# A two-layer network on one core: the second layer's experts in engine loops, its tokens sorted in three parts, with eight weight and row buffers

## The chip, the cores and the metric

The kernel runs on one core of a Trainium2 chip. Its time is the device time of one execution in microseconds (us); smaller is better. The engines are TensorE (PE in the profile, its weight loads PEld), VectorE (DVE), ScalarE (ACT), GpSimd (POOL) and SyncE (SP), which here only issues transfers. Each engine runs its own instruction stream in order and waits on semaphores.

## The reference

Two layers run on a tensor x of 8 x 512 tokens with 128 features, 4096 tokens in all. Layer 0 is a recurrent scan over every second token and a small mixture of experts; layer 1 is an attention with 16 heads and relative positions and then a larger mixture of experts. Only that last part is touched. Cut to what matters:

```python
h = _layernorm(x) * (1 + cb) + sb
# _L1_ffn_ref, 8 experts, the best 2 of each token, and one shared expert for all
scores = softmax(xt @ gate_w.T)
idx = top_k(scores + gate_b, 2)[1]
weights = take_along_axis(scores, idx)
cw = sum(one_hot(idx, 8) * weights[..., None], axis=1)
h1 = einsum('td,efd->etf', xt, w1) + b1
h3 = einsum('td,efd->etf', xt, w3) + b3
a = swiglu(h1 * h3)          # g * sigmoid(1.702 g) * (l + 1) on even and odd columns, clipped at 7
y = einsum('etf,edf->etd', a, w2) + b2
routed = einsum('te,etd->td', cw, y)
shared = swiglu((xt @ sw1.T + sb1) * (xt @ sw3.T + sb3)) @ sw2.T + sb2
x = x + gb * (routed + shared)
```

All is float32.

## The kernel before

`program` runs the stages one after the other. The last one is `experts1` (L1397). It does not compute all 8 experts for all tokens. It sorts: each token's two (token, expert) pairs get a slot in a buffer in HBM, ordered by expert, and the experts run over blocks of `SLOTS` = 256 slots that all belong to one expert.

**Routing.** VectorE makes softmax, the two maxima and the running counts, and from these the slot of every pair (`pos`, L1698) and the expert of every block (`eid`). The 32 tiles of 128 tokens are sorted in `PARTS` = 2 parts of `PT` = 16 tiles (2048 tokens). A part has at most `RB` = 2*16*128/256 + 7 = 23 blocks, since each of the 8 experts may leave one block unfilled. So 46 routed blocks run, always, beside `NSHARED` = 16 blocks of the shared expert, which need no sorting: N = 62.

**Order.** `ORDER` puts 11 shared blocks first, then the 46 routed ones, then the last 5 shared ones. All engines follow it; their code is written out block by block.

**GpSimd** scatters the rows of `norm.h` to `sorted_h` with one indirect DMA for each tile and each of its two experts (64 in all, L1565). For each part it then waits until all its results are stored and gathers them to `got` the same way (32 for each part, L1574). A ring of `NGOT` = 4 semaphores lets it run four tiles ahead of their landing.

**SyncE** serves the routed blocks. For block m it first issues the rows of block m + 1 (`load_slots`, L1525, 128 KB, `NX` = 4 buffers), then reads the expert's number into a register (L1516) and issues the weights of block m (`load_weights`, L1517, 320 KB, `NW` = 5 buffers, free when block m - 5 has left `down`), then stores the result of block m - 5 (`store`, L1531, 128 KB).

**One block** is a pipeline over four engines. TensorE: `turn` (two transposes of the rows, L1829), `up` (four matmuls of 256 columns, L1842 to L1851, to one PSUM bank each), and two blocks later `down` (L1866; for shared blocks also L1865, the output bias). ScalarE: `slots` (L1592), `gate` (L1598), `tanh` (L1610), `lin` (L1604), `take` (L1621). VectorE: `gates` (L1725, L1728), `join` of the block before (L1742, L1748), `lins` (L1733, L1736). `select_biases` (L1709 to L1720) picks the first biases of all routed blocks on VectorE, once, at block 4.

**The end.** `combine(k)` (L1754) adds the two gathered rows of tile k, weighted, to `acc`: two operations of 128 x 128. Eight tiles of part 0 are combined between the blocks, one every second block; the other 24 after the last block, with `finish` (L1760, L1762) for every four tiles, and SyncE stores each of the eight pieces of the output (L1546).

## Time and profile before

| | us |
|---|---|
| median of 3 runs (1836.76 to 1840.22) | 1839.58 |
| the profiled execution | 1833.77 |
| its span, first to last instruction | 1832.0 |
| its granted TensorE clock, mean | 0.877 |

The shares of the whole span say little here, since the stages have different limits. `experts1` is its last 390 us or so. What is of use is a table of stretches (busy time of each engine, the clock granted to TensorE, the share of the DMA engines), the number of blocks in each, and single instructions in order of time where an engine stands still. In a row of the timeline the bracket tells how long the engine had been idle and what released it; "remote" means that a semaphore changed at that moment, and that no instruction of that moment had changed it.

### The profile page before, as it was taken

The numbers are of one execution on the slowest core, as the hardware profiler recorded it, in microseconds if no ns is written. First come the engines' busy times: TensorE is split into PE (matmuls) and PEld (weight loads), VectorE is DVE, ScalarE is ACT, GpSimd is POOL, SyncE is SP. The second block draws the span as 40 slices with busy tenths as digits, with TensorE's granted clock in tenths as the row PEclk, the third lists the DMA queues.
The fourth block names the chain that finished last, engine by engine and source line by source line (L and its number), as shares of the span: only waits on it lengthen the run. The fifth ranks groups of instructions, "written<-read, shape, count | busy, mean of one in ns | idle before, by whom it ended". The sixth has DMA issues, their size and how long they took to land. (4 is left out here: it accounts for less than half of the span.)

```text
span 1832.0 us, 41747 instructions
## 1 busy us (share of the span) xinstructions
PE 1461.2 (80%) x15040; PEld 996.7 (54%) x15040; DVE 1314.7 (72%) x3621; ACT 952.3 (52%) x2202; POOL 592.0 (32%) x584
## 2 busy tenths in 40 slices
PE   4277767776698569999999999999999577198490
PEld 2277667776643235555555555555555455187370
DVE  6899999997678736667666676666766685077286
ACT  7555555554311436666666666666666432066260
POOL 0876666770113334111111111111110107601415
PEclk7688888888699789999999999999999867599695
DMA  2400000000000012111111111111110001258352
GB/s 70 132 1 1 1 1 1 1 1 0 12 1 5 15 22 42 31 29 30 29 30 26 25 30 28 30 30 30 30 28 8 15 1 54 71 154 231 95 140 82
DMA packets 150357, 71.53 MB, mean 39 GB/s; under 512 B 95234, under 2 KB 135700, under 8 KB 150164
## 3 DMA queue, kind: packets, MB, share of 16 engines
q1 hardware_dynamic: 143316, 60.42, 15.1%
q0 software_dynamic: 4096, 8.40, 1.5%
q8 instruction: 106, 1.74, 0.4%
q14 instruction: 87, 0.71, 0.1%
q10 hardware_dynamic: 2752, 0.26, 0.1%
HBM read 38.11 MB, written 18.35 MB: 31 GB/s over the span
## 5 line engine op out<-in xcount | busy, mean ns | idle before, releaser
L1299 DVE TENSOR_REDUCE ntop<-score 128x1 f32<-128x512 f32 x512 | 317.9, 683 | 252.0 <-PE score L1178 252.0
L1256 ACT ACTIVATE prob<-score,ntop 128x512 f32<-128x512 f32 x512 | 317.5, 688 | 268.6 <-DVE ntop L1299 268.6
L440 ACT ACTIVATE hist<-zp 128x168 f32<-128x168 f32 (+1 forms) x768 | 224.4, 313 | 171.1 <-DVE zp L408 170.4
L1214 PE MATMUL turned<-ident,prob 128*128 128x128 f32 x2048 | 268.5, 280 | 1.8 <-DVE probT L1240 1.8
L490 PEld LDWEIGHTS py<-hist,diagC 128*128 128x128 f32 x2048 | 262.6, 214 | 0.0
L490 PE MATMUL py<-hist,diagC 128*128 128x128 f32 x2048 | 262.3, 296 | 0.0
L1178 PE MATMUL score<-ks,qs 64*128 64x512 f32 x1024 | 255.0, 616 | 0.0
L1214 PEld LDWEIGHTS turned<-ident,prob 128*128 128x128 f32 x2048 | 219.0, 141 | 49.1 <-issue 28.1
L460 POOL TENSOR_TENSOR xb<-xc,Bm 128x1024 f32<-128x1024 f32 x128 | 244.9, 1954 | 1.3
L403 DVE TENSOR_TENSOR gp<-hist,Ap 128x168 f32<-128x168 f32 (+1 forms) x768 | 229.7, 328 | 14.8 <-POOL xb L460 14.8
L408 DVE TENSOR_TENSOR zp<-gp,xb 128x168 f32<-128x168 f32 (+1 forms) x768 | 232.9, 333 | 0.0
L1240 ACT COPY probT<-turned 128x512 f32<-128x512 f32 x384 | 198.7, 595 | 1.2 <-PE turned L1214 1.2
L1178 PEld LDWEIGHTS score<-ks,qs 64*128 64x128 f32 x1024 | 88.5, 186 | 168.8 <-issue 168.8
L931 POOL TENSOR_TENSOR qr<-rel_q,own_shift 128x256 f32<-128x256 f32 x64 | 37.3, 615 | 403.9 <-PE score L1178 373.0
L1174 PE MATMUL score<-tb,qr 32*32 32x512 f32 x4096 | 148.6, 603 | 12.4 <-PEq L946 11.7
L1198 PEld LDWEIGHTS mixed<-probT,vh 128*16 128x16 f32 x4096 | 100.7, 96 | 95.8 <-issue 95.8
L1198 PE MATMUL mixed<-probT,vh 128*16 128x128 f32 x4096 | 136.4, 274 | 0.7 <-issue 0.7
L938 POOL TENSOR_TENSOR qs<-key_q,own_batch 128x256 f32<-128x256 f32 x128 | 95.6, 792 | 73.5 <-DMA key_q<-q_sb 73.5
L1574 POOL DMA_INDIRECT got<-sorted_y,pos x64 | 61.9, 966 | 160.5 <-DMA sorted_y<-ysb 141.6
L1286 DVE RECIPROCAL inv<-cm 128x256 f32<-128x256 f32 x64 | 111.5, 1743 | 0.0
L1240 DVE COPY probT<-turned 128x512 f32<-128x512 f32 x128 | 88.5, 691 | 0.1
L1565 POOL DMA_INDIRECT sorted_h<-hz,pos x64 | 63.7, 995 | 55.9 <-DVE pos L1698 36.7
(304 smaller groups left out, 1624.9 us busy)
## 6 DMA issues: line engine op xcount, KB each, us to landing
w<-in_ew SPq DMA_DIRECT2D x46, 320.0 KB
tb<-in_table SPq DMA_DIRECT2D x64, 127.1 KB
sorted_h<-nought SPq DMA_DIRECT2D x2, 2944.0 KB, 17.2
xs<-sorted_h SPq DMA_DIRECT2D x46, 128.0 KB
sorted_y<-ysb SPq DMA_DIRECT2D x46, 128.0 KB
ks<-k_sb SPq DMA_DIRECT2D x32, 128.0 KB
rel_q<-q_sb SPq DMA_DIRECT2D x248, 8.0 KB
key_q<-q_sb SPq DMA_DIRECT2D x248, 8.0 KB
```

What stands on the lines that cost most here:

```text
L403: v.tensor_tensor(g[:, lo:hi], prev[:, lo:hi], Ap[:, lo:hi], ALU.mult).then_inc(decayed, 1)
L408: v.tensor_tensor(zp[j][:, 0:hi - lo], g[:, lo:hi], xb[:, par, u, lo:hi], ALU.add)\
L440: nc.scalar.activation(hist[:, par, u, lo:hi], zp[j][:, 0:hi - lo], ACT.Tanh)\
L460: nc.gpsimd.tensor_tensor(xb[:, par, u:u + XB_STEPS, :].rearrange("p u (s b) -> p u s b", b=NB), xc[:, par, u * NB:(u + XB_STEPS) * NB].re ...
L490: last = mm(py[par][:, 0:P], diagC[:, s, :], hist[:, par, :, s * NB:(s + 1) * NB], start=False, stop=(s == NS - 1))
L1174: mm(score_ps[r][32 * w:32 * w + 32, :], qr[p][rows, w, g, :, :].rearrange("p b v -> p (b v)"), tb[p][rows, s:s + SEQ], start=True, stop=F ...
L1178: mm(score_ps[r][:, :], qs[p][rows, r % 2, g, :, :, :].rearrange("p w b v -> p (w b v)"), ks[p][rows, :], start=False, stop=True).then_inc ...
L1198: last = mm(mixed_ps[32 * c:32 * c + SUMS, bh * P:(bh + 1) * P], vh[:, p, j, b, :], probT[G // 2 % 2][:, j, :, :].rearrange("p t (w b v) - ...
L1214: last = nc.tensor.transpose(turned_ps[BANK[e]][:, j * P:(j + 1) * P], prob[G % 2][e][:, j * P:(j + 1) * P], ident[:, :])
L1240: copy(probT[G // 2 % 2][:, :, G % 2 * GRP + TURN[e], :], turned_ps[BANK[e]][:, :].rearrange("p (j t) -> p j t", j=JT))\
L1256: nc.scalar.activation(prob[G % 2][e][:, :], score_ps[r][:, :], ACT.Exp, bias=ntop[:, G % 2, e:e + 1]).then_inc(prob_ready, 1)
L1299: v.tensor_reduce(ntop[:, G % 2, e:e + 1], score_ps[r][:, :], AX.X, ALU.max, negate=True)\
```

## The change

The change is confined to `experts1`, its constants, and the width of the zeroed buffers; one transfer in `attention` gets another semaphore.

- **Parts.** The tiles are sorted in three parts of 8, 16 and 8 tiles (1024, 2048 and 1024 tokens). `RB` is 15, 23 and 15, so 53 routed blocks run, and N = 69. The running counts are made for groups of 8 tiles in 3 steps and joined for the middle part; their totals come from three small matmuls of their own.
- **Order.** 10 shared blocks first, 53 routed, 6 shared last.
- **SyncE.** Eight weight buffers and eight row buffers. The first 8 loads of weights are issued before any rows; then, for block m, the weights of block m + 8, the store of block m, the rows of block m + 8. The weights land on one semaphore for each group of four.
- **Loops.** TensorE runs blocks 12 to 59 in 6 laps of 8 blocks, ScalarE blocks 4 to 7 in 2 laps and 16 to 59 in 11 laps of 4, VectorE blocks 4 to 61 in laps of 2, five loops with 3 + 15 + 4 + 3 + 4 = 29 laps. Semaphore values and the columns of biases and tiles are worked out in registers.
- **Biases.** The first biases are picked by four small matmuls (`select` on TensorE, at block 2) and one copy on ScalarE.
- **Combines.** Tiles 0 to 7 are combined at blocks 40 to 47, tiles 8 to 15 at blocks 54 to 61, one for every block. Tiles 16 to 31 and all `finish` come after the last block, behind a wait for the last `take`. `NGOT` is 2.

```diff
-PARTS = 2
-PT = NT // PARTS
-RB = 2 * PT * P // SLOTS + NE1 - 1
-NROUTED = PARTS * RB
+QT = 8
+PART_QUARTERS = (1, 2, 1)
+PARTS = len(PART_QUARTERS)
+PT = [QT * q for q in PART_QUARTERS]
+RB = [2 * t * P // SLOTS + NE1 - 1 for t in PT]
+NROUTED = R0[PARTS]
...
-    NW, NX, NY, NGOT = 5, 4, 4, 4
-    SHARED_FIRST, SELECT_AT, IN_LOOP, EVERY = 11, 4, 8, 2
+    NW, WG, NX, NY, NGOT = 8, 4, 8, 4, 2
+    LAP = 8
+    SHARED_FIRST = 10
+    SELECT_AT = 2
...
-            load_slots(0)
-            for m in range(NROUTED):
-                if m + 1 < NROUTED:
-                    load_slots(m + 1)
-                load_weights(m)
-                if m >= AFTER:
-                    store(m - AFTER)
-            for m in range(NROUTED - AFTER, NROUTED):
-                store(m)
+            for m in range(NW):
+                load_weights(m)
+            for m in range(SLOTS_AHEAD):
+                load_slots(m)
+            for m in range(NROUTED):
+                if m + NW < NROUTED:
+                    load_weights(m + NW)
+                store(m)
+                for k in range(SLOTS_AHEAD, NROUTED):
+                    if asked_at(k) == m:
+                        load_slots(k)
...
             for s in range(PARTS):
                 for i in range(NY):
-                    pool.wait_ge(y_out[i], 16 * stores(i, (s + 1) * RB))
-                for k in range(s * PT, (s + 1) * PT):
+                    pool.wait_ge(y_out[i], 16 * stores(i, R0[s + 1]))
+                for k in range(T0[s], T0[s + 1]):
...
+            def stretch(n0, turns, tile=None):
+                with dve.Fori(0, turns) as i:
+                    for u in range(2):
+                        q = (n0 + u) % 2
+                        bias = routed_bias(2 * i + (n0 - SHARED_FIRST + u))
+                        gates(2 * i + (n0 + u), q, bias)
+                        join(2 * i + (n0 - 1 + u), 1 - q)
+                        lins(2 * i + (n0 + u), q, bias)
+                        if tile is not None:
+                            combine(2 * i + (tile + u), (tile + u) % NGOT, i + (tile // NGOT + 1))
...
+            dve.wait_ge(sel_ready, 1)
+            stretch(SHARED_FIRST, 15)
+            dve.wait_ge(y_taken, SHARED_FIRST)
+            stretch(SHARED_FIRST + 30, 4, 0)
+            stretch(SHARED_FIRST + 38, 3)
+            stretch(SHARED_FIRST + 44, 4, 8)
+            for n in range(SHARED_FIRST + 52, N):
+                gates(n, n % 2, bias_of(n))
+                join(n - 1, (n - 1) % 2)
+                lins(n, n % 2, bias_of(n))
+            join(N - 1, (N - 1) % 2)
+            dve.wait_ge(y_taken, N)
+            for k in range(16, NT):
+                combine(k, k % NGOT, k // NGOT + 1)
...
+            with pe.Fori(0, 6) as i:
+                for u in range(LAP):
+                    q = u % 2
+                    turn(LAP * i + (3 + u), (3 + u) % NX, 1 - q, i + ((3 + u) // NX + 1))
+                    up_routed(LAP * i + (12 + u), LAP * i + (2 + u), (2 + u) % NW, q, WG * i + WG * ((2 + u) // NW + 1))
+                    down(LAP * i + (10 + u), q, W[u])
```

Three places of the order show what moves. On VectorE, the end of a routed block with a combine behind it reads like this before (`gg`, `ll`, `a` are the block's tiles, `acc` the sum of a token tile, `got` the gathered rows; the brackets name the semaphores waited for):

```order
L1742 SCALAR_TENSOR_TENSOR ll<-ll,gg 128x256 [waits ll_ready,gg_ready]
L1748 SCALAR_TENSOR_TENSOR a<-th,ll 128x256 [waits y_ready1,th_ready,gl_ready]
L1733 SCALAR_TENSOR_TENSOR ll<-pz,b_sel,l 128x256 [waits first_l]
L1736 TENSOR_SCALAR ll<-ll 128x256 [waits ll_raw]
L1754 SCALAR_TENSOR_TENSOR acc<-got,wt,acc 128x128 [waits got_in0,y_taken]
L1754 SCALAR_TENSOR_TENSOR acc<-got,wt,acc 128x128 [waits combined]
L1725 SCALAR_TENSOR_TENSOR gg<-pz,b_sel,g 128x256 [waits first_g,combined]
```

and like this inside the loop of the changed kernel, up to the end of the combine, where ISA and REGISTER_ALU are register instructions:

```order
L1801 SCALAR_TENSOR_TENSOR a<-th,ll 128x256 [waits y_ready1]
L1787 ISA [waits first_l]
L1787 SCALAR_TENSOR_TENSOR ll<-pz,b_sel,l 128x256
L1790 TENSOR_SCALAR ll<-ll 128x256 [waits ll_raw]
L1807 ISA
L1812 ISA [waits got_in0]
L1812 ISA
L1812 SCALAR_TENSOR_TENSOR acc<-got,wt,acc 128x128
L1813 REGISTER_ALU
L1812 ISA [waits combined]
L1812 SCALAR_TENSOR_TENSOR acc<-got,wt,acc 128x128
L1813 REGISTER_ALU
```

The operations and their order are the same; seven register instructions stand between them in this piece, three of them with a wait. On SyncE, the steady rows for one routed block are before:

```order
L1525 DMA xs3<-sorted_h1 128x2x128 [waits xs_turned]
L1516 TENSOR_LOAD eid [waits y_ready1]
L1516 ISA x2
L1517 ISA
L1517 DMA w1_1<-in_ew1 128x640
L1531 DMA sorted_y0<-ysb1 128x2x128 [waits y_taken]
```

and in the changed kernel:

```order
L1541 TENSOR_LOAD eid [waits y_ready1]
L1541 ISA x2
L1542 ISA
L1542 DMA w1_2<-in_ew1 128x640
L1562 DMA sorted_y1<-ysb2 128x2x128 [waits y_taken]
L1555 DMA xs2<-sorted_h1 128x2x128 [waits xs_turned]
```

The rows are now asked for after the store, and the store is that of the block whose `down` has just ended. On GpSimd, the changed kernel scatters the three parts and begins the gathers of the first, which is of 8 tiles (16 DMAs) now:

```order
L1598 DMA sorted_h0<-hz,pos 3840x128 [waits pos_ready]
L1598 DMA sorted_h0<-hz,pos 3840x128 x15
L1598 DMA sorted_h1<-hz,pos 5888x128 x32
L1598 DMA sorted_h2<-hz,pos 3840x128 x16
L1607 DMA got<-sorted_y0,pos 128x128 [waits y_out2,y_out3,y_out1,y_out0]
L1607 DMA got<-sorted_y0,pos 128x128 x3
L1607 DMA got<-sorted_y0,pos 128x128 [waits got_in0]
L1607 DMA got<-sorted_y0,pos 128x128
L1607 DMA got<-sorted_y0,pos 128x128 [waits got_in1]
```

Before, `sorted_h0` and `sorted_h1` took 32 DMAs each, the first eight gathers waited for no landing, and the ring had four semaphores. Now four gathers (two tiles) start without such a wait.

## Rows read from the trace of the kernel before

**Rows 1.** Stretches, `tanh` alone: us, ACT busy (x, one a block), PEclk, DMA share, GB/s

```profile
1511.00:1537.00 26.00, 2.44 (x6) 0.87 0.14 47
1537.00:1602.50 65.50, 0.81 (x2) 0.55 0.22 69
1602.50:1619.30 16.80, 1.63 (x4) 0.72 0.22 63
1619.30:1683.00 63.70, 10.17 (x25) 1.00 0.82 216
1683.00:1729.00 46.00, 1.63 (x4) 0.65 0.39 107
1729.00:1776.00 47.00, 7.34 (x18) 0.94 0.65 173
1776.00:1832.00 56.00, 1.23 (x3) 0.59 0.25 75
```

**Rows 2.** Lines L1565 and L1574: ns min/median/max, first and last start

```profile
L1565 POOL DMA_INDIRECT sorted_h<-hz,pos x64: 954/959/1847, 1511.4 to 1593.2; - x64
...
L1574 POOL DMA_INDIRECT got<-sorted_y,pos x64: 940/945/1181, 1683.0 to 1815.6; - x64
```

**Rows 3.** Timeline in the scatter, PE and ACT: start, us, instruction, idle before

```profile
1541.80 0.49 PE L1866 MATMUL pz<-w_shared,a 128*128 128x128 f32 x2
...
1550.06 0.47 ACT L1604 ACTIVATE l<-pz,b_all 128x256 f32<-128x256 f32 x1 [6.24 <-remote]
...
1570.36 0.37 ACT L1621 COPY acc<-pz 128x256 f32<-128x256 f32 x1 [19.83 <-remote]
```

**Rows 4.** SyncE's register move of line L1517, whole span: ns min/median/max

```profile
L1517 SPq MOVE w<-in_ew x46: 3/29/1388, 1560.5 to 1761.1; - x46
```

**Rows 5.** The stretch 1619.3 to 1683, busy of PE, PEld, DVE, ACT, POOL

```profile
1619.30:1683.00 63.70, 62.20 (x351) 53.53 (x350) 55.62 (x150) 46.45 (x126) 0.00 (x0) 1.00 0.82 216
```

**Rows 6.** The chain that ended last, 1602 to 1683: start, us, what

```profile
1625.28 0.43 PE pz L1842 x2
...
1627.71 0.43 PE pz L1842 x2
...
1678.43 3.32 DMA w<-in_ew
```

**Rows 7.** VectorE's timeline, a block without and one with a combine

```profile
1741.38 0.48 DVE L1725 SCALAR_TENSOR_TENSOR gg<-pz,b_sel,g 128x256 f32<-128x256 f32 x1
...
1743.63 0.48 DVE L1725 SCALAR_TENSOR_TENSOR gg<-pz,b_sel,g 128x256 f32<-128x256 f32 x1
...
1745.86 0.73 DVE L1754 SCALAR_TENSOR_TENSOR acc<-got,wt,acc 128x128 f32<-128x128 f32 x2
1746.63 0.48 DVE L1725 SCALAR_TENSOR_TENSOR gg<-pz,b_sel,g 128x256 f32<-128x256 f32 x1
```

**Rows 8.** Groups of lines, 1450 to 1832, `select_biases`

```profile
L1716 DVE TENSOR_TENSOR b_prod<-done,b_all 128x368 f32<-128x368 f32 x4 | 3.0, 798 | 0.0
...
L1719 DVE TENSOR_REDUCE b_sel<-b_prod 128x184 f32<-128x1472 f32 x1 | 1.7, 1687 | 0.0
```

**Rows 9.** The scan's loops: register rows, the branch, VectorE's idle time before L403

```profile
L402 DVEq FUSED_REGOPS  x192: 57/57/65, 148.4 to 444.2; - x192
...
L360 PEldq COMPARE_BRANCH  x7: 76/207/230, 169.4 to 464.1; - x7
...
L403 DVE TENSOR_TENSOR gp<-hist,Ap 128x168 f32<-128x168 f32 x563 | 168.5, 329 | 13.2 <-POOL xb L460 13.2
```

**Rows 10.** Timeline after the last block: PE, ACT, VectorE

```profile
1789.37 0.80 PE L1866 MATMUL pz<-w_shared,a 128*128 128x128 f32 x2
...
1811.25 0.37 ACT L1621 COPY acc<-pz 128x256 f32<-128x256 f32 x1 [17.86 <-remote]
...
1828.91 0.69 DVE L1762 TENSOR_TENSOR x<-x,acc 128x512 f32<-128x512 f32 x1
```

**Rows 11.** DMA queues, 155 to 470 (the scan): packets, MB, share

```profile
q14 instruction: 28, 0.23, 0.2%
```

More of the change, by code:

```diff
@@ L1624, in _ @@
-            for n in range(N + 2):
-                if n + 1 < N and ORDER[n + 1][0] == "routed":
-                    slots(ORDER[n + 1][1])
-                if n < N:
-                    if n == SHARED_FIRST:
-                        act.wait_ge(eid_ready, 2)
-                    gate(n)
-                if 1 <= n <= N:
-                    tanh(n - 1)
-                if n < N:
-                    lin(n)
-                if n >= 2:
-                    take(n - 2)
+                if not (isinstance(n, int) and n < 2):
+                    act.wait_ge(gg_raw, n - 1)
@@ new lines, in take, with take_shared, take_routed @@
+            def take(n, q, dst):
+                act.wait_ge(y_ready, n + 1)
+                A.copy(dst, Y[q][:, 0:SLOTS]).then_inc(y_taken, 1)
+            def take_shared(n, q, i):
+                dst = acc[:, i * HALVES:(i + 1) * HALVES, :] if isinstance(i, int) else acc[:, bass.ds(i * HALVES, HALVES), :]
+                take(n, q, dst.rearrange("p o e -> p (o e)"))
+            def take_routed(n, q, slot, laps):
+                if not (isinstance(laps, int) and laps == 0):
+                    act.wait_ge(y_out[slot], 16 * laps)
+                take(n, q, ysb[slot][:, :, :].rearrange("p o e -> p (o e)"))
@@ new lines, in _ @@
+            act.wait_ge(w_in, 16 * 5)
+            for n in range(0, 4):
+                if n == SELECT_AT + 1:
+                    act.wait_ge(spots_ps, 2)
+                    A.copy(b1_sel[:, :, :].rearrange("p c m -> p (c m)"), XT[0][:, 0:4 * NROUTED]).then_inc(sel_ready, 1)
+                block_step(n)
+            with act.Fori(0, 2) as i:
+                for u in range(2):
+                    gate(2 * i + (4 + u), u, shared_bias)
+                    tanh(2 * i + (3 + u), 1 - u)
+                    lin(2 * i + (4 + u), u, shared_bias)
+                    take_shared(2 * i + (2 + u), u, 2 * i + (2 + u))
@@ new lines, in _ @@
+            for n in range(8, 16):
+                if n == SHARED_FIRST:
+                    act.wait_ge(sel_ready, 1)
+                block_step(n)
+            with act.Fori(0, 11) as i:
+                for u in range(NY):
+                    q = u % 2
+                    n, m = NY * i + (16 + u), NY * i + (NY + 2 + u)
+                    slots(NY * i + (NY + 3 + u), 1 - q)
+                    gate(n, q, routed_bias(m))
+                    tanh(NY * i + (16 - 1 + u), 1 - q)
+                    lin(n, q, routed_bias(m))
+                    take_routed(NY * i + (16 - 2 + u), q, u, i + 1)
@@ L1638, in _ @@
+            for n in range(60, N + 2):
+                block_step(n)
         @block.vector
@@ L1785, in _ @@
                 if k % TPB == TPB - 1:
+                    if k // TPB == 4:
+                        for j in range(4):
+                            finish(j)
                     finish(k // TPB)
@@ L1790, in _ @@
             mm = nc.tensor.matmul
-            pe.wait_ge(w_in, 16 * 4)
+            pe.wait_ge(w_in, 16 * 5)
             def logits(j):
@@ L1868, in down @@
-                last.then_inc(y_ready, 1)
-            for n in range(N + 2):
-                if n + 1 < N and ORDER[n + 1][0] == "routed":
-                    turn(ORDER[n + 1][1])
-                if n < N:
-                    up(n)
-                if n >= 2:
-                    down(n - 2)
+                    if seeded:
+                        k = shared_block * HALVES + o
+                        mm(Y[q][:, cols], cwT[:, k * P:(k + 1) * P], b2[:, :], start=True, stop=False)
+                    last = mm(Y[q][:, cols], a[:, q, cols], w[:, 4 * P:5 * P], start=not seeded, stop=True)
@@ new lines, in down, with block_step @@
+                last.then_inc(y_ready, 1)
+            def block_step(n):
+                if n + 1 < N and ORDER[n + 1][0] == "routed":
+                    m = ORDER[n + 1][1]
+                    turn(m, m % NX, m % 2, ring(m, NX))
+                if n < N:
+                    kind, m = ORDER[n]
+                    if kind == "shared":
+                        up(n, Wsh, hT[:, m * SLOTS:(m + 1) * SLOTS])
+                    else:
+                        up_routed(n, m, m % NW, m % 2, group_loads(m))
+                if n >= 2:
+                    kind, m = ORDER[n - 2]
+                    if kind == "shared":
+                        down(n - 2, n % 2, Wsh, m)
+                    else:
+                        down(n - 2, n % 2, W[m % NW])
@@ new lines, in select @@
+            def select():
+                pe.wait_ge(eid_ready, 2)
+                for c in range(4):
+                    last = mm(XT[0][:, c * NROUTED:(c + 1) * NROUTED],
+                              b1_rows[:, :].rearrange("e (p c) -> e c p", c=4)[:, c, :], mine[:, :],
+                              start=True, stop=True)
+                last.then_inc(spots_ps, 1)
+            for n in range(0, 12):
+                if n == SELECT_AT:
+                    select()
+                if n + 1 == SHARED_FIRST:
+                    pe.wait_ge(sel_ready, 1)
+                block_step(n)
```

322 lines of the change are left out of this document (162 added, 160 removed).

## The prediction

> **What bounds the kernel now.** I read the stage first by stretches, with the number of blocks in each [rows 1]: one `tanh` is one block. The reader should see two paces. In 1619.3 to 1683 there are 25 blocks in 63.7 us, 2.55 each; in 1537 to 1602.5 there are 2 in 65.5 us, and in 1683 to 1729 there are 4 in 46. The clock falls to 0.55 and 0.65 there because TensorE has nothing to do. The slow stretches are those of GpSimd's indirect DMAs [rows 2]: 64 scatters from 1511.4 to 1593.2, 1.3 us apart, then 32 gathers from 1683.0 on and 32 more at the end, up to 1815.6.
>
> What stands still is seen in order of time [rows 3]. TensorE ends a `down` at 1542.3; the `take` that waits for it starts at 1570.36, 28 us later, released by a semaphore at a moment when TensorE does nothing. So the signal is late, not the work. SyncE has the same trouble: a register move of 29 ns takes up to 1388 ns [rows 4], as long as one indirect DMA. What the messages queue behind I can't see; that they do while GpSimd issues is in the rows. It does not set in at once: of the 82 us of scatters the first 26 still hold 6 blocks, and in the gathers at 1683 about two blocks pass before the stand. It ends some 6 to 8 us after the last issue (1593.2 to about 1602).
>
> In the fast stretch TensorE is busy 62.2 of 63.7 us [rows 5] and VectorE 55.6. The pace without waits is 2.43 us, from one block's first matmul to the next one's [rows 6]. There are four waits for weights between 1619 and 1683, of which one stands in [rows 6]: the weights of a block are asked for only one row load ahead of their use.
>
> **The sum,** against the profiled execution's 1833.77 us (span 1832.0), which is 5.8 below the median.
>
> *Seven more blocks.* 53 routed instead of 46, at 2.43 us [rows 6]: +17.0. Nothing hides them: TensorE is full in that stage.
>
> *A third burst in the middle.* The scatter keeps its 64 DMAs. Before, 32 gathers lie between blocks and 32 at the end; now 16 and 32 lie between blocks and 16 at the end. The burst of 32 took 46.0 us with 4 blocks in it [rows 1], so it cost 46.0 - 4 x 2.43 = 36.3. It remains. One of 16 is 20 us shorter and should hold 3 blocks: 26 - 7.3 = 18.7; I take +17. The bounds are 0 (the first 26 us of the scatter still made blocks) and 26.
>
> *The end.* From the first gather to the end it was 1776 to 1832, 56 us [rows 1]. Now all combines of tiles 16 to 31 and all `finish` wait for the last `take`. That one was at 1811.25, 21 us after TensorE's last matmul had ended (1789.37 + 0.80) [rows 10]: its signal was late too. The gathers now take 20 us and the queue 6 more to empty: 26. Then 32 operations of a combine at 0.385 (0.77 for a tile, 1745.86 to 1746.63 [rows 7]) make 12.3, sixteen operations of 0.69 + 0.03 [rows 10] make 11.5, and the last store 3.1 (1828.9 to 1832): 53. So -3. If the last signal is in time, some 14 us after the first gather as its matmul is now (1790.2 - 1776), the end is 41; with the 35 us that the signal took before (1811.25 - 1776) it is 62.
>
> *Waits for weights and rows.* With weights and rows of eight blocks there, the slow start behind the scatter (4 blocks in 16.8 us, [rows 1], against some 11 at the low clock) gives back 6, and the waits in the fast stretch 63.7 - 25 x 2.43 = 3: -9, with 0 and -13 as ends. The DMA engines are at 0.82 there [rows 1]; one block moves 576 KB before and after, so 2.43 us is near what they bear, and I don't go lower than TensorE's pace. Before rows come, SyncE issues eight loads of weights, five instructions each; at 1.4 us apiece [rows 4] that is 56 us, still inside the 91 of the scatter.
>
> *Biases.* `select_biases` leaves VectorE: 4 x 0.798 + 1.687 = 4.9 us and one small operation [rows 8]. It lay between blocks of the first 26 us; that lets one block more through before the stand: -2.4, ends -5 and 0. The four small matmuls and the copy that replace it wait for `mine`, ready long before block 2.
>
> *Combines.* Without a combine VectorE can make a block in 2.25 us, with one in 3.0 (1741.38, 1743.63, 1746.63 in [rows 7]). Before, eight combines stood at every second block: 5.25 for two blocks against 4.86, +0.4 each, 3 in all. Now sixteen stand at every block of their stretches, so VectorE becomes the bound: 3.0 + registers instead of 2.43. Each has seven more register instructions. The nearest row has them at 57 ns, and in the scan's loops they cost VectorE no idle time, 13.2 us on 563 operations, all put to GpSimd [rows 9]. But there they pass under a running operation, while here some stand behind a wait for the operation before. I take 0.3 of the 0.4 they would make: 16 x (3.3 - 2.43) = 14, less 3: +11. The ends are +6 (3.0) and +16 (0.6 for the registers).
>
> *Registers in the other looped blocks.* VectorE has 2.43 - 2.25 = 0.18 to spare. Three register instructions behind a wait, 0.17, and half a branch, 0.1 (TensorE's takes 0.207 [rows 9]), make 2.52. On 28 such blocks +3, ends 0 and +8.
>
> The sum: 17.0 + 17 - 3 - 9 - 2.4 + 11 + 3 = +33.6, rounded down to +32 for what the pieces share at their seams: 1833.8 + 32 = 1865.8 for the profiled execution, 1839.6 + 32 = 1871.6 for the median. I forecast **1870**. What a measurement can tell from no change is about 0.2%, 3.7 us.
>
> **A rule about loops.** In the scan, whose loops take 7 laps (the x7 in [rows 9]), the small instruction transfers are 28 [rows 11]: four a lap, so a lap does bring code anew, and VectorE shows no idle time put to it. Their price by these rows is about nothing. The Trainium skill ("Runtime: NRT & Kernel Launch", instruction fetch mechanics) says that a taken branch to a target outside the two pages held must wait for a transfer of that page, and that kernels therefore prefer unrolled code; the bodies here are far shorter than the scan's, and the trace agrees with the transfers but not with the stall. By that rule the sum would be that of rival D.
>
> **The rivals.**
>
> *A, faster: the stand goes.* GpSimd may run only two tiles ahead instead of four. If its queue is what holds the signals up, a shorter one lets them pass, and both middle bursts cost little: 1870 - 17 - 36 = 1817. For it: the stand sets in late, so something fills first. Against: the scatter has no limit in either kernel, and in the gathers before a limit of four tiles changed neither their pace of 1.3 us nor the stand. If it decides, it does so in the burst of 32 behind block 47.
>
> *B, the short burst is over before the stand.* Only the 17 us go: 1853. For it: 6 blocks in the scatter's first 26 us. Against: two in the gathers at 1683.
>
> *C, the blocks run on in the scatter too.* Without `select_biases` and with less code the first stretch might make all ten shared blocks: some 8 blocks and 20 us more on top of A, 1797. Nothing in the rows of SyncE or TensorE speaks for it.
>
> *D, much slower: the branches stall.* 29 laps on VectorE, each with a transfer and an idle time of 1 to 2 us: +29 to +58, 1899 to 1928. It decides if VectorE's idle time appears at every second block. Against it are [rows 9].
>
> *E, the waits for weights stay,* since the DMA engines are full: +9, 1879, inside the range.
>
> **How the numbers follow.** The forecast with E 0.56, B 0.12, A 0.17, C 0.05, D 0.05, and 0.05 for terms that cancel out near 1840. Slower: 0.56 + 0.12 + 0.05 = 0.73. Faster: 0.17 + 0.05 and 0.01 of the last, 0.23. The same: 0.04. The range: upward the ends of combines, registers and weights, 5 + 5 + 9, and the rest of the end, make 1893; downward it takes in A with 1815. C, D and what is left of the others are outside, under 2 in 10. So 1815 to 1893; the likeliest case alone has 1850 to 1893.
>
> **What the next profile would show.** Right: a stand of about 37 us behind block 47 and one of about 17 behind block 24, `take` released without a TensorE instruction beside it, the low clock there; 3.2 to 3.4 us a block where combines stand, with VectorE busy throughout; hardly a wait for weights; the last `take` about 26 us after the first gather of the third part. Wrong: if blocks go on at 2.5 us beside the gathers (A), if the stretch at block 24 has no stand (B), if VectorE idles at each lap (D), or if the first ten blocks end before the scatter does (C).

## The result: slower, and what the profile after shows

The changed kernel takes **1900.16 us** (median of 4 runs, 1898.95 to 1902.42) against 1838.51 for the kernel before on the same chip. The ratio is 1.0337, with a 95% interval of 1.0319 to 1.0355. The profiled execution has a span of 1899.2 us against 1832.0, so 67.2 us are to be found there. By the medians it is 61.7 us (the profiled execution of the kernel before was its fastest, that of the changed kernel its slowest). The forecast was 1870, some 31 us more, its range 1815 to 1893: the sign was right, the size was half.

The stretches of the profile after, `tanh` alone, as in [rows 1] (a `tanh` is one block; columns: start:end, length, ScalarE busy (count), granted clock, DMA share, GB/s; for 1.00 the clock is 2.4 GHz, for 0.50 it is 1.2):

```profile
1512.90:1538.20 25.30, 0.81 (x2) 0.79 0.54 167
1538.20:1603.70 65.50, 0.82 (x3) 0.50 0.18 56
1603.70:1633.40 29.70, 3.28 (x9) 0.84 0.00 1
1633.40:1681.30 47.90, 6.48 (x16) 0.93 0.70 187
1681.30:1709.30 28.00, 1.68 (x5) 0.76 0.53 143
1709.30:1733.10 23.80, 3.62 (x10) 1.00 0.83 222
1733.10:1759.30 26.20, 2.84 (x8) 1.00 0.60 159
...
1765.70:1811.90 46.20, 1.22 (x3) 0.62 0.35 97
1811.90:1846.10 34.20, 4.48 (x11) 0.91 0.28 81
1846.10:1899.20 53.10, 1.64 (x4) 0.62 0.18 59
```

And GpSimd's two lines (ns min/median/max, first and last start), which answer [rows 2]:

```profile
L1598 POOL DMA_INDIRECT sorted_h<-hz,pos x64: 954/958/1212, 1512.9 to 1593.1; - x64
...
L1607 POOL DMA_INDIRECT got<-sorted_y,pos x64: 938/944/1192, 1681.3 to 1865.1; - x64
```

Three pieces add up to the 67.2 us:

- From the first scatter to the block of index 12: 1512.9 to 1633.4 = 120.5 us, before 1511.4 to 1619.3 = 107.9. With 1.5 for the later first scatter that is **+14.1**. The forecast had -8.4 there (-2.4 and the ramp's -6), so 22.5 of the miss lie here. Four blocks begin before the last scatter is out, before it was eight [rows 1].
- From there to the first gather of the last part: 212.7 us, before 156.7: **+56.0**. The forecast had 17 + 17 - 3 + 11 + 3 = 45, so 11 lie here.
- From there to the end: 53.1 us, before 56.0: **-2.9**, forecast -3.

What the stand is made of can be read on ScalarE's timeline of the changed kernel (start, us, instruction, idle before and releaser). It waits each time for a signal of TensorE:

```profile
1522.21 0.47 ACT L1637 ACTIVATE l<-pz,b_shared 128x256 f32<-128x256 f32 x1 [1.70 <-issue]
1530.78 0.37 ACT L1647 COPY acc<-pz 128x256 f32<-128x256 f32 x1 [8.09 <-issue]
...
1537.84 0.47 ACT L1631 ACTIVATE g<-pz,b_shared 128x256 f32<-128x256 f32 x1 [6.45 <-issue]
...
1549.04 0.47 ACT L1637 ACTIVATE l<-pz,b_shared 128x256 f32<-128x256 f32 x1 [10.42 <-remote]
1570.73 0.37 ACT L1647 COPY acc<-pz 128x256 f32<-128x256 f32 x1 [21.23 <-remote]
1582.03 0.47 ACT L1631 ACTIVATE g<-pz,b_shared 128x256 f32<-128x256 f32 x1 [10.92 <-remote]
...
1593.14 0.47 ACT L1637 ACTIVATE l<-pz,b_shared 128x256 f32<-128x256 f32 x1 [10.33 <-remote]
1603.05 0.37 ACT L1647 COPY acc<-pz 128x256 f32 x1 [9.44 <-remote]
```

The signals from 1549 on come 21.7, 11.3 and 11.1 us apart. Between the `lin` and the `take` TensorE has eight matmuls with eight weight loads (a `down` of a shared block), between a `take` and the next `gate` and between `gate` and `lin` four with four. 21.7 / 16 = 1.36, 11.3 / 8 = 1.41, 11.1 / 8 = 1.39: counted this way, one TensorE instruction gets through in 1.4 us, and the price of a block beside the scatters is its number of TensorE instructions, 32 for a shared block, 45 us. In [rows 3] the same sixteen lie between 1550.06 and 1570.36: 20.3 / 16 = 1.27. The routed blocks beside the second burst of gathers give a second count, since their `down` has four matmuls with four loads:

```profile
1798.76 0.47 ACT L1637 ACTIVATE l<-pz,b_sel 128x256 f32<-128x256 f32 x1 [8.41 <-remote]
1809.91 0.37 ACT L1647 COPY ysb<-pz 128x256 f32<-128x256 f32 x1 [10.68 <-remote]
```

Here the `take` comes 11.15 us behind the `lin`, half of 21.7, and 11.15 / 8 is 1.39 again; so in these rows the delay goes with the number of instructions and is not a fixed time for a `take`. The signals before these two, also eight instructions apart, took 7.2 and 9.2 us: the pace of 1.4 us is reached only 25 to 35 us after a burst of DMAs has begun.

The second loss is one wait for rows, on the chain that ended last:

```profile
1662.07 3.32 DMA xs<-sorted_h
```

and on TensorE's timeline, where it also costs the clock (L1911, a pair of matmuls, takes 1.06 us behind it, and took 0.60 at 1657.81):

```profile
1659.78 0.61 PE L1939 MATMUL pz<-w,a 128*128 128x128 f32 x4
1665.43 0.69 PE L1905 MATMUL pz<-ident,xs 128*128 128x128 f32 x2 [5.04 <-DMA xs<-sorted_h]
1665.91 1.06 PE L1911 MATMUL pz<-xT,w 128*128 128x256 f32 x2
```

The rows of the second part are not asked for before SyncE has stored block 11 of the first (`SECOND_AT`), so they arrive too late.

The third is VectorE's pace where combines stand: 8 blocks in 26.2 us, 3.7 for one (from `gates` at 1735.18 to the next at 1738.80 it is 3.62). Between operations there is time now that [rows 7] don't have:

```profile
1734.31 0.35 DVE L1812 SCALAR_TENSOR_TENSOR acc<-got,wt,acc  x1 [0.18 <-DVE acc L1812]
1735.18 0.48 DVE L1780 SCALAR_TENSOR_TENSOR gg<-pz,b_sel,g 128x256 f32<-128x256 f32 x1 [0.53 <-DVE acc L1812]
...
1738.21 0.35 DVE L1812 SCALAR_TENSOR_TENSOR acc<-got,wt,acc  x1 [0.19 <-DVE acc L1812]
1738.80 0.48 DVE L1780 SCALAR_TENSOR_TENSOR gg<-pz,b_sel,g 128x256 f32<-128x256 f32 x1 [0.23 <-DVE acc L1812]
```

### The profile page after: what moved, and what is told of

The parts are those of the page before. It is cut to its first block and busy times, and to the rows that moved or that the text cites. A ratio compares the mean times of both kernels' runs of the same rounds, so it can differ in the third digit from the quotient of the medians.

```text
span 1899.2 us, 42862 instructions
## 1 busy us (share of the span) xinstructions
PE 1498.1 (79%) x15148; PEld 1014.7 (53%) x15148; DVE 1327.4 (70%) x3659; ACT 965.4 (51%) x2238; POOL 589.5 (31%) x585
## 3 DMA queue, kind: packets, MB, share of 16 engines
q1 hardware_dynamic: 148932, 65.47, 15.3%
## 5 line engine op out<-in xcount | busy, mean ns | idle before, releaser
L410 DVE TENSOR_TENSOR gp<-hist,Ap 128x168 f32<-128x168 f32 (+1 forms) x768 | 231.2, 331 | 15.3 <-POOL xb L467 15.3
```

The source lines that it names most:

```text
L410: v.tensor_tensor(g[:, lo:hi], prev[:, lo:hi], Ap[:, lo:hi], ALU.mult).then_inc(decayed, 1)
```

## The experiments

Eighteen runs were made in seven groups, each group on one chip together with the kernel before. That kernel's own time tells two sorts of groups apart, and the traces kept from a group, of whatever kernel without pauses, agree with it:

| group | kernel before, us | blocks beside the scatters |
|---|---|---|
| the kernels' own times | 1838.51 | stand |
| e1 to e4 | 1749.36 | run on |
| e5 to e8 | 1747.95 | run on |
| e9 to e12 | 1747.09 | run on |
| e13, e14 | 1834.94 | stand |
| e15, e16 | 1744.78 | run on |
| e17 | 1746.43 | run on |
| e18 | 1833.05 | (only the kernel with pauses was traced; by the time of the kernel before: stand) |

So the stand, 90 us of the kernel before, is not a fixed property of the program. Whether it belongs to a chip, its host or something that changes there in time isn't known: two groups, e9 to e12 and e13 to e14, carry the same chip number, one without and one with it. In no group do executions of both sorts occur. Below, "with stands" and "without" mean these.

### Without stands: what the change itself costs

The changed kernel again, and the kernel before for its trace.

> The changed kernel as it is, since the chip of the first four experiments was another one than that of the two kernels' own times: there the kernel before took 1749 instead of 1839 us, and the blocks ran on at 3.4 us beside scatters and gathers, so the stands were missing. On a chip without stands: seven more blocks at 2.43 (17), 0.7 us of registers on sixteen blocks with a combine (11), 0.2 on the others (6), less the waits that went (9): 1749 - 9 + 34 - 15 (no select_biases, an end with 16 gathers instead of 32) = about 1760, ratio 1.003 to 1.009. On a chip with stands: 1900, ratio 1.033, as before.

> The kernel before as it is, for its trace on the same chip as the runs beside it. On a chip without stands it is near 1749 us: its 11 blocks ahead of the routed ones end within some 45 us of the first scatter, and the last take comes within 15 us of the first gather of the end. On a chip with stands 1839 and the trace shown of before.

Measured: 1762.97 us, ratio 1.0091 (1.0074 to 1.0108); the kernel before 1748.94 in its eight executions of e6, 1747.95 over the group. The total of 1760 was met to 3 us; how far its terms were met is said below. The stretches of the changed kernel, then of the kernel before, `tanh` alone:

```profile
1511.00:1548.00 37.00, 4.06 (x11) 1.00 0.48 152
```

```profile
1511.00:1525.40 14.40, 1.63 (x4) 1.00 0.14 47
1525.40:1549.00 23.60, 1.63 (x4) 0.57 0.15 50
```

Here 11 blocks lie in the first 37 us of the changed kernel and eight in the 38 us of the kernel before. There, the biases' select takes VectorE's time; TensorE, busy until then, waits 2.3 us for it, and behind the wait the granted clock is at its lower level (0.57 over the stretch), as the next rows show (a pair of matmuls takes 1.06 us and not 0.60):

```profile
1525.23 0.60 PE L1842 MATMUL pz<-hTz,w_shared 128*128 128x256 f32 x2
1528.13 1.09 PE L1845 MATMUL pz<-hTz,w_shared 128*128 128x256 f32 x2 [2.30 <-DVE gg L1725]
1529.01 1.06 PE L1848 MATMUL pz<-hTz,w_shared 128*128 128x256 f32 x2
```

At the block of index 12 the changed kernel is 19.6 us ahead (1554.0 against 1573.6), and still ends behind.

**Loops written out,** all engines:

```diff
-            with act.Fori(0, 11) as i:
+            for i in range(11):
```

> The changed kernel with every engine's loop written out: the same instructions in the same order, no branches and no registers. The prediction's terms say 0.3 us on each of sixteen blocks with a combine (5) and 0.09 on 28 others (3): 1899 - 8 = 1891. Theory D (branches that wait for code) would give 1899 - 29 or more: 1870 or less. If the 3.66 us of a block with a combine is VectorE's own work and not its registers, and the registers pass beside work: 1897 to 1900.

Measured: 1748.36 us, ratio 0.9979 (0.9952 to 1.0006), against 1.0091: the loops cost 15 us by the medians, 20 by the ratios, about twice the 8 expected. (In the group of e1 to e4 six of the 19 executions of the kernel before took 1757 to 1764 us and the others 1745 to 1750, which draws the ratios of that group down; the medians and the two spans, 15.3 us apart, say 15.) Two blocks with a combine on VectorE, with loops (the changed kernel of the group above) and without:

```profile
1644.77 0.48 DVE L1780 SCALAR_TENSOR_TENSOR gg<-pz,b_sel,g 128x256 f32<-128x256 f32 x1 [0.23 <-DVE acc L1812]
...
1647.72 0.35 DVE L1812 SCALAR_TENSOR_TENSOR acc<-got,wt,acc  x1 [0.18 <-DVE acc L1812]
1648.60 0.48 DVE L1780 SCALAR_TENSOR_TENSOR gg<-pz,b_sel,g 128x256 f32<-128x256 f32 x1 [0.53 <-DVE acc L1812]
...
1652.21 0.48 DVE L1780 SCALAR_TENSOR_TENSOR gg<-pz,b_sel,g 128x256 f32<-128x256 f32 x1 [0.23 <-DVE acc L1812]
```

```profile
1639.90 0.48 DVE L1780 SCALAR_TENSOR_TENSOR gg<-pz,b_sel,g 128x256 f32<-128x256 f32 x1
...
1642.92 0.48 DVE L1780 SCALAR_TENSOR_TENSOR gg<-pz,b_sel,g 128x256 f32<-128x256 f32 x1
...
1645.93 0.48 DVE L1780 SCALAR_TENSOR_TENSOR gg<-pz,b_sel,g 128x256 f32<-128x256 f32 x1
```

7.44 us for two blocks with loops, 6.03 without: 0.7 a block. 0.53 + 0.23 us of it stand before `gates` of two blocks and 0.18 before each second half of a combine. The 0.53 stands where a lap begins, so a lap costs 0.3 us more than a block inside it. Sixteen blocks make 11; blocks 12 to 39, without combines, take 79.4 us with loops and 75.4 without, which is the other 4.

**Rows asked for earlier:**

```diff
-                return max(m - SLOTS_AHEAD, SECOND_AT) if PART_OF[m] == 1 else m - SLOTS_AHEAD
+                return m - SLOTS_AHEAD
```

> The changed kernel without the rule that no row load of the second part is asked for before block 11 of the first: each is asked for eight blocks ahead. One block (the 24th) waited 9 us for rows there, with 8 to 9 us of TensorE idle. If that wait is a loss of its own: 1899 - 7 = 1892, and the blocks behind it keep their 2.5 us. If the DMA engines are what is full there: the wait moves to other blocks and 1897 to 1901 results.

Measured: 1754.79 us, ratio 1.0018 (0.9988 to 1.0047): some 8 us less than the changed kernel by the medians (13 by the ratios, with the same reservation; the two are of different groups). Blocks 20 to 26 are 2.4 to 2.9 us apart; the wait is gone, not moved.

**Both repairs:**

> The changed kernel with both repairs that the earlier runs priced apart: the loops written out (they cost 15 us: 1748 against 1763) and the rows of the second part asked for eight blocks ahead (8 us: 1755 against 1763). If the two are independent, as the places are (registers on VectorE where combines stand; one wait for rows at block 23): 1763 - 15 - 8 = 1740, ratio to the kernel before 0.995, faster than both. If the row wait only moves: 1745 to 1749. On a chip with stands: 1900 - 16 - 9 = 1875, ratio 1.02.

Measured: 1742.87 us, ratio **0.9971** (0.9956 to 0.9986): faster than the kernel before, without stands, by 0.3%. 3 us less was gained than the sum; TensorE waits 1.5 and 1.9 us for weights at blocks 21 and 25, waits that e4 alone doesn't have.

**Two parts again:** `PART_QUARTERS = (2, 2)`, everything written out, sixteen tiles combined behind blocks 44 to 59.

> The changed kernel written out, with two parts of 2048 tokens (46 routed blocks, as before) in place of three; sixteen tiles combined behind blocks 44 to 59, one a block. It undoes the third part and the loops together; the loops alone are undone in another run. With stands: 1900 - 17 (seven blocks) - 15 (burst of 16 in the middle) + 3 (32 gathers in one burst either way, the end as in before, 56 instead of 53) - 10 (loops) = about 1861. Without stands, against the written-out kernel with three parts (1748): seven blocks less, 17, and 16 more gathers at the end, some 20 us more before the last combine: about 1745 to 1752.

Measured: 1756.09 us, ratio 1.0057 (1.0036 to 1.0078), above the 1745 to 1752 expected: without stands the third part is worth some 8 us in the written-out kernel, in spite of its seven blocks. In its trace the `tanh` of index 7 and 8 are 19 us apart (1539.0 and 1558.1), since 32 scatters must land before the first routed block and not 16, and from the first gather of the last part (1702.9) to the end (1753.9) it is 51 us, against 37 with three parts (1705.9 to 1742.6).

**No bias matmuls** in `down` of the shared blocks (the seed of PSUM left out):

```diff
-                seeded = shared_block is not None
+                seeded = False
```

> The changed kernel without the matmuls of the second bias and the weights of the sixteen shared blocks (each down of a shared block has four matmul instructions instead of eight; the output lacks the term of the second bias). With stands, theory M (TensorE's signals queue behind its own instructions, one of them in 1.4 us while GpSimd issues: the takes of blocks 3, 4 and 5 came 21.7 us behind the signal before when 16 loads and matmuls lay between, 11.2 when 8 did): the take of such a block comes 11 instead of 21.7 us after the signal before it, one or two blocks more begin beside the scatter, 1900 - 16 x 0.85 (matmuls) - 5 = about 1881. If signals are late by time and not by instructions, the spacing of 21.7 us stays. Without stands: 16 x 0.85 us less TensorE time on shared blocks of 3.4 to 3.6 us, but VectorE's 2.4 us and the scatter's 82 us bound them: 5 to 13 us less.

> As the run without the bias matmuls (the output lacks the term of the second bias), in case this chip has stands. Then theory M (one load or matmul of TensorE passes in 1.4 us) wants the take of a shared block 11 us behind the signal before it, not 21.7, and a total near 1881. On a chip without stands: 1748, as measured.

Measured: 1748.33 and 1748.42 us, 14.6 less than the changed kernel, where 5 to 13 was expected. It is 16 x 0.9: a shared block costs 2.5 us instead of 3.4. Both groups were without stands, so these runs say nothing on theory M; it rests on the two counts above, of 16 and of 8 instructions.

**Weights later.** First all loads behind the last scatter, then only behind the first part's sixteen:

```diff
+            sp.wait_ge(scattered[PARTS - 1], 16 * 2 * PT[PARTS - 1])
             for m in range(NW):
```

> The changed kernel, with SyncE's first eight weight loads and eight row loads held back until the last scatter has landed. In the changed kernel the stand of the blocks beside the scatters begins after three blocks (some 10 us after the first scatter), in the kernel before after six (some 30 us). Theory L (the 2.6 MB of weights and SyncE's forty instructions, which now run beside the first scatters, bring the stand forward): seven or eight blocks begin before the last scatter instead of four, three or four blocks at 3.6 us are saved, less some 6 us for loads that are then late: 1899 - 14 + 6 = about 1891. Theory S (the eight small matmuls that select the biases stand in TensorE's row of messages, and the stand begins where VectorE leaves GpSimd alone): still three to five blocks, and the late loads cost 3 to 10 us: 1903 to 1909.

> The changed kernel, with the first eight weight loads held back only until the sixteen scatters of the first part have landed, some 20 us, when the rows can be read anyway. On a chip with stands theory L (SyncE's early loads bring the stand forward from 26 to 8 us after the first scatter) says that five or six blocks begin in the first 26 us, as in the kernel before, and not three: 10 to 14 us less than 1900. Theory S (the sixteen instructions of the select, in TensorE's row of signals): no change, 1900. On a chip without stands only the late weights are felt: block 10 begins near 1549 and its weights come by then, 0 to +3 us on 1763.

Measured: 1827.86 (ratio 1.043, 1.0367 to 1.0492) and 1768.62 us (1.0112). My expectation of the first was made for stands and was off by 60 us without them: the routed blocks then wait for their rows until 1611. The second costs 6 us, where 0 to 3 was expected. It was run twice more, to meet stands, and did not:

> The changed kernel with the first weight loads held back until the sixteen scatters of the first part have landed, for a session with stands (changed kernel 1900, four blocks begun before the last scatter). Theory L (SyncE's loads in the first 20 us bring the stand forward): five blocks or six begin in the first 26 us instead of three, 1886 to 1892. Theory S (the select's sixteen instructions on TensorE and the missing hold-up of GpSimd by VectorE): three or four as before, 1898 to 1903. In a session without stands: 1768, as measured.

> The changed kernel with the first weight loads held back until the sixteen scatters of the first part have landed, for a session with stands (before near 1835, changed 1900, four blocks begun before the last scatter has landed; the kernel before without its select, six). Theory L (SyncE's early loads take the other two blocks): six begin, 1886 to 1892. Theory S (the select's sixteen instructions on TensorE take them): four, 1898 to 1903. In a session without stands: 1768, as measured.

Measured: 1769.26 and 1769.36 us.

### With stands: what makes them

**VectorE's loops alone written out:**

> The changed kernel with only VectorE's loops written out; TensorE and ScalarE keep theirs. Writing all three out saved 15 us. The prediction puts the price on VectorE (0.3 us a block with a combine, 0.09 on the others). The rows of the run without loops show blocks with a combine 3.0 us apart, with loops 3.75. If VectorE's registers make that, 12 to 15 us go here too: about 1749, ratio 1.001. If TensorE's or ScalarE's registers and branches hold the blocks up, less than 5 go: 1758 or more.

Measured: 1880.83 us, ratio 1.0221 (1.0156 to 1.0287), against 1.0337: 1.2% or 21 us less, though the intervals allow 6 to 36. The traces are closer: the span is 16.3 us shorter than the changed kernel's (1882.9 against 1899.2), and writing out all loops shortened it by 15.3 without stands. So VectorE's loops, registers and the step from lap to lap, are the price as far as the traces show, and TensorE's and ScalarE's cost nothing that shows. The blocks beside the scatters begin as in the changed kernel (1515.7, 1519.7, 1537.7, 1581.2, 1603.2), and its combines are 3.0 us apart.

**The kernel before without its select on VectorE:**

```diff
-                chain(v.tensor_tensor(mine, ...
-                for c in range(4): ...
-                v.tensor_reduce(bsel[:, :, :], bprod[:, :, :, :], AX.X, ALU.add).then_inc(eid_ready, 1)
+                v.memset(bsel[:, :, :], 0.0).then_inc(eid_ready, 1)
```

> The kernel before, with select_biases replaced by a memset of the biases (the output lacks the routed experts' first biases). On chips without stands TensorE waits 2.6 us for VectorE there, the granted clock goes from 1.00 to 0.57, and blocks 4 to 8 are 6.3 us apart instead of 3.4. Theory K (the select costs its own 4.9 us and, by the clock behind it, some 12 us more): blocks 4 to 8 begin 3.4 us apart, but the routed blocks still cannot begin before the rows of the first part have landed (near 1555), so that 4 to 8 us are left of it: about 1741. If the select costs only its own time: 1744 to 1747, and the blocks stay 6.3 us apart.

Measured: 1838.52 us, ratio 1.0004 (0.9974 to 1.0035). It met stands, so its expectation of the clock can't be judged. But it shows more: 5 us of VectorE's work and TensorE's wait for it are gone, and nothing is gained (the interval allows 5 us less to 6 more). The `tanh` begin at 1517.6, 1519.3, 1523.4, 1529.2, 1544.7, 1588.1 and 1605.2: six before the last scatter and not eight. Counted from the first scatter (1511.36 before, 1514.40 here) the first four are at the same times to 0.1 us, the fifth comes 12 us later, and the block of index 12 comes at 114.8 us against 108.0. What also changed is GpSimd's pace. Kernel before, then this one, GpSimd's timeline (start, us for one scatter; 3.0 us are to be added to the first to compare it with the second):

```profile
1522.16 0.96 POOL L1565 DMA_INDIRECT sorted_h<-hz,pos  x1 [0.30 <-issue]
1523.42 1.54 POOL L1565 DMA_INDIRECT sorted_h<-hz,pos  x1 [0.31 <-issue]
1525.26 1.85 POOL L1565 DMA_INDIRECT sorted_h<-hz,pos  x1 [0.30 <-issue]
1527.41 0.96 POOL L1565 DMA_INDIRECT sorted_h<-hz,pos  x1 [0.30 <-issue]
```

```profile
1523.93 0.96 POOL L1565 DMA_INDIRECT sorted_h<-hz,pos  x1 [0.30 <-issue]
1525.19 0.96 POOL L1565 DMA_INDIRECT sorted_h<-hz,pos  x1 [0.31 <-issue]
1526.46 0.95 POOL L1565 DMA_INDIRECT sorted_h<-hz,pos  x1 [0.30 <-issue]
```

and what VectorE does at 1523 in the kernel before:

```profile
1523.30 2.97 DVE L1716 TENSOR_TENSOR b_prod<-done,b_all 128x368 f32<-128x368 f32 x4
1526.30 1.69 DVE L1719 TENSOR_REDUCE b_sel<-b_prod 128x184 f32<-128x1472 f32 x1
```

The two scatters beside the TENSOR_TENSOR were held up, by 0.6 and 0.9 us; the one at 1527.41, beside the TENSOR_REDUCE, was not. Without stands it is the same (e6: 1.54 and 1.86 us), so the hold-up is the select's doing and not the stand's. The Trainium skill ("SBUF — State Buffer", who interferes with whom) says that a VectorE instruction with two inputs in SBUF contends with a GpSimd instruction that reads SBUF, and the two stretched scatters agree. It also says that a probe saw neither `tensor_tensor` nor `tensor_reduce` stall a DMA; for `tensor_reduce` the trace agrees, for `tensor_tensor` it shows the contrary.

That the hold-up gave the signals time is the reading that fits the next experiment. It isn't shown by itself: the select also kept VectorE busy, so that fewer signals came in that time.

**A pause behind each indirect DMA:**

```diff
+            def pause(i):
+                g.memset(idle[:, :], 0.0).then_inc(consts, 1)
+                pool.wait_ge(consts, CONSTS + i + 1)
```

> The changed kernel, with a 0.52 us memset of a scratch tile on GpSimd behind each of its 128 indirect DMAs, so that they are issued some 1.9 us apart instead of 1.26. Theory P (signals pile up only while GpSimd issues without a break, as in the 26 us in which VectorE held it up now and then in the kernel before): the stands go, the blocks beside scatters and gathers run at 2.5 to 3.7 us each, the scatters end some 40 us later but do not hold up blocks: 1899 - 60 (stands of the scatter, net) - 37 - 15 (middle bursts) + 12 (last burst longer) = about 1800. Rival (each indirect DMA holds signals up by its number, whatever the spacing, or for as long as any is under way): the stands last longer, 82 to 122 us in the scatter and 20 + 41 + 20 to 30 + 61 + 30 us in the gathers: 1899 + 40 + 10 + 20 + 10 = about 1980.

> As the run with a 0.52 us memset behind each indirect DMA, in case this chip has stands. Theory P (a break of half a microsecond lets the signals through) then wants blocks beside the scatters at 3.4 us and a total near 1800, far below 1900; if the number of DMAs decides, about 1980. On a chip without stands: 1788, as measured.

> The changed kernel with a 0.52 us memset behind each indirect DMA, for a session with stands (kernel before near 1835). The run before showed that the select on VectorE, which stretched two scatters to 1.54 and 1.85 us, put the stand off by two blocks: without it the stand came 10 us after the first scatter. Theory P (signals get through when GpSimd is held up): with 0.8 us more between any two, blocks run at 3.4 to 4 us beside the scatters and the total is 1800 to 1830, below the kernel before. Rival N (each indirect DMA costs the signals its share, however far apart): the stand lasts as long as the scatters, now 120 us: about 1980.

> As the run with a 0.52 us memset behind each indirect DMA, once more for a session with stands (kernel before near 1835). Theory P (a break lets the signals through): 1800 to 1830. Rival N (each indirect DMA costs the signals its share): about 1980. Without stands 1788, as measured.

Measured without stands: 1787.77, 1787.92 and 1790.19 us, 25 us more than the changed kernel (in the traces 7 of them are a longer wait for rows at block 23). In the group of e18, where the kernel before took 1833.05: **1786.26 us**. The same program takes the same time in both sorts of groups, 47 us less than the kernel before and 114 less than the changed kernel with stands. GpSimd and ScalarE in that run:

```profile
1514.81 0.96 POOL L1604 DMA_INDIRECT sorted_h<-hz,pos  x1 [0.28 <-POOL idle L1597]
1515.77 0.55 POOL L1597 MEMSET idle<- 128x512 f32 x1
1516.60 0.96 POOL L1604 DMA_INDIRECT sorted_h<-hz,pos  x1 [0.28 <-POOL idle L1597]
```

```profile
1524.23 0.37 ACT L1655 COPY acc<-pz 128x256 f32<-128x256 f32 x1 [1.19 <-PE pz L1947]
1525.18 0.47 ACT L1639 ACTIVATE g<-pz,b_shared 128x256 f32<-128x256 f32 x1 [0.58 <-PE pz L1922]
```

The scatters are 1.79 us apart instead of 1.26, no idle time of ScalarE beside them ends with "remote", the longer ones all end with a TensorE instruction of that moment, and ten blocks begin by 1550. Theory P had the direction right and asked for 1800 to 1830; rival N is out. It is one execution of each kernel there, and that this group had stands is known only from the one of the kernel before; the difference is far above what executions of one kernel differ by within a group here. Three things come with the pause, the gap between two DMAs, perhaps fewer of them under way at a time, and GpSimd's own wait for its memset; no run tells them apart.

## Why the prediction was wrong in size

Against the profiled execution the forecast was +32 to +33.6, measured +67.2. Right were the blocks, the bursts of gathers and the end. What failed, in order of size: the scatter, which the sum took as unchanged but for gains of 2.4 and 6 us and which became 14.1 us longer (points 2 and 3); the waits, of which one was overlooked (4); and the registers (5).

1. **Seven more blocks, the bursts, the end** (17 + 17 - 3): held. The burst of 16 took 22.6 us for three blocks (1682.9 to 1705.5), 22.6 - 7.3 = 15.3 against 17. The one of 32 held 1811.9 - 1767.6 = 44.3 us for three blocks, 37 against 36.3 before. The end took 53.1 against 53, the last `take` came 27 us after its first gather against 26.
2. **"Biases ... lets one block more through before the stand: -2.4"** is the step that failed most, with the sign wrong. I had costed the select's 4.9 us as if they only delayed blocks. The run without it shows that the select's absence costs two blocks beside the scatters, 6.8 us up to the block of index 12, as much as it gives; that this goes by way of GpSimd, which the select had held up, is argued. And the replacement may not be free where signals queue: its eight matmuls are 16 more TensorE instructions, 22 us at 1.4 us each if they stand in the queue; no run shows how much of it is paid.
3. **The ramp, -6**, failed with it. What was left to do when the scatters were out was not routed blocks that wait for weights, but six shared ones, which need none: 29.7 us for eight blocks in the profile after, 3.7 each, the first of them at a low clock. Points 2 and 3 are 22.5 us. The other two of the four blocks lost beside the scatters, 5.7 us up to the block of index 12 (120.5 against 114.8), remain open between the select's 16 instructions and SyncE's early loads: the run that would tell them apart never met stands.
4. **Waits, -3**: the waits for weights went, but a wait for rows came at block 23 (`tanh` at 1659.3 and 1668.4; 8 us by its experiment), which I could have read from `SECOND_AT`: I took buffers of eight as rows of eight ahead.
5. **Combines, 3.3 us a block**: 3.66 in the profile. I took 0.3 of 0.4 us for the registers; they are 0.7 in the runs with and without loops: seven instructions of 57 ns would be 0.4, but the idle times that stand behind a combine's operations, where the next one or its registers wait for it, are 0.18, 0.23 and 0.53 us. Sixteen blocks make +6. The other looped blocks cost 4 against 3.
6. **Rival D** (branches stall) gave 1899 to 1928, and the time came out at 1899. It is still wrong: writing VectorE's loops out shortens the span by 16 us, not 29 to 58, and the longest idle time at a lap in the combine stretches is 0.53 us, 0.3 more than inside one, not 1 to 2. A rival isn't confirmed by its total. The rule of the Trainium skill on branches that was set beside it would need a stall at each lap that this trace doesn't show.
7. **Rival A** (the stand goes with `NGOT` 2) fell: with two tiles ahead the burst of 32 stood as before. Yet its root, that the stand depends on how GpSimd issues, was right, as the one run with pauses shows. B fell with the burst of 16, which did stand, and C with the scatters, beside which four blocks began and not ten.

The base of the sum had the stands in it. Without them 1760 was expected, with the registers already resized to 0.7 and 0.2 by the first runs, and 1763 was measured. That the total closes to 3 us is luck. From the traces of e5 and e6 the changed kernel is 30 us better up to the block of index 12 and in the end together (19.6 and 10.6), where the terms had 21, and loses 40.6 us in between, where they had 31. Two misses of 9 us cancel; most of the second is the wait for rows.

## What to carry to other kernels

Where a trace shows one engine's signals late while another issues indirect DMAs back to back, try a pause of half a microsecond between them (here 114 us gained in the one execution with late signals, 25 us lost without), and count the instructions of the engine whose signals are late, not its time. Removing work that looks like pure delay can gain nothing, so ask of every removed operation whom it held up. And time a kernel in more than one session: here a change was 3.4% slower in one and 0.9% in another, and the paused version was ahead in one only.

## What the hardware showed that I had not expected

- The same kernel takes 1748 or 1836 us, by the group of runs, and what the traces show of it is late signals beside GpSimd's indirect DMAs.
- With stands one TensorE instruction passes in 1.4 us and SyncE's register move takes up to 1388 ns [rows 4]; with a pause, 0.53 us more between indirect DMAs, one execution shows none of it.
- Each execution here is traced. The Trainium skill ("NOTIFIC — the notification-queue block", overflow: three behaviours, one of which stalls the engine) describes how the records that instructions leave pass a block that holds the engines back when its inner queue is full. That would fit a price for each instruction, register moves too, and a limit that differs from one group of runs to another; no run here shows it, and it is only argued.
- In e6 TensorE, busy before and after, waited 2.3 us once, and the granted clock, 1.00 up to there, was 0.57 over the next 23.6 us.
